# Two normalisation loops of a transformer layer, issued one and two tiles apart

## What is computed

```python
def _layernorm(x, axis=-1, eps=1e-5):
    m = jnp.mean(x, axis=axis, keepdims=True)
    v = jnp.var(x, axis=axis, keepdims=True)
    return (x - m) / jnp.sqrt(v + eps)
# attention: 16 heads of 64, causal, rope on q and k
qkv = einsum('bsd,ed->bse', x, W_qkv)
out = softmax(mask(rope(q) @ rope(k).T / 8)) @ v
return einsum('bsd,ed->bse', out, W_o)
# feed-forward: the input is normalised a second time inside
z = (x - mu) * rsqrt(var + EPS) * ln_g + ln_b
z_sent = mean(z, axis=1)
z_bn = (z_sent - bn_mean) * rsqrt(bn_var + EPS) * bn_g + bn_b
probs = softmax(z_bn @ Wr + br); idx = argmax(probs); gate = probs[idx]
h = relu(z @ W_down[idx] + b_down[idx])
y = (h @ W_up[idx] + b_up[idx]) * gate
# layer
x = x + attention(_layernorm(x))
x = x + ffn(_layernorm(x), ...)
```

## Time and profile before

| | us |
|---|---|
| median of 2 runs | 6524.79 |
| lowest, highest | 6509.48, 6540.09 |
| the profiled execution | 6517.81 |
| span of its slowest core (core 3) | 6516.3 |
| span of its fastest core (core 6) | 6481.7 |

### The profile page before, as it was taken

The page is one execution under the profiler, slowest core; times in us unless marked ns, Lnnn a source line. Parts: engine busy times, 40 slices in busy tenths (PEclk is TensorE's granted clock), DMA queues, the critical chain, the costliest instruction groups (busy, mean ns, idle before and its releaser), DMA issues. The chain is left out here.

```text
span 6516.3 us, 47310 instructions; the slowest of 8 cores (6481.7 to 6516.3 us)
## 1 busy us (share of the span) xinstructions
PE 4396.2 (67%) x11412; PEld 1075.9 (17%) x11412; DVE 2256.1 (35%) x2561; ACT 1701.7 (26%) x1983; POOL 1428.2 (22%) x1736
## 2 busy tenths in 40 slices
PE   0166888885346788888335688888634678888833
PEld 0022111111112111112002211111201221111200
DVE  1244323333434333333343433333334433332334
ACT  0000444430000244442000044444000014444300
POOL 0027000002225400000340810000123460000033
PEclk9989555556568755556557955555656985555655
DMA  5310000001021000002021100000202100000101
GB/s 140 113 36 17 1 0 1 1 30 39 16 100 28 9 1 1 1 0 68 0 87 42 23 1 1 1 1 1 68 2 105 34 12 1 0 1 1 62 7 62
DMA packets 151776, 180.51 MB, mean 28 GB/s; under 512 B 89951, under 2 KB 110559, under 8 KB 151015
## 3 DMA queue, kind: packets, MB, share of 16 engines
q1 hardware_dynamic: 151532, 177.48, 8.8%
HBM read 133.41 MB, written 44.04 MB: 27 GB/s over the span
## 5 line engine op out<-in xcount | busy, mean ns | idle before, releaser
L578 ACT ACTIVATE PT<-pss,ecol_s 128x1024 bf16<-128x1024 f32 x1280 | 1426.7, 1115 | 2451.2 <-PE pss L560 2447.2
L525 DVE RECIPROCAL rb<-po 64x512 f32<-64x512 f32 x256 | 859.9, 3359 | 2229.4 <-PE po L515 2229.4
L560 PE MATMUL pss<-qkT 64*128 64x512 bf16 x2560 | 1315.6, 616 | 0.0
L493 PE MATMUL po<-PT,v 128*65 128x512 bf16 (+3 forms) x2560 | 1225.0, 565 | 35.7 <-POOL PT L593 34.2
L593 POOL TENSOR_SCALAR_AFFINE_SELECT PT<-PT 128x128 bf16<-128x128 bf16 x1024 | 274.7, 292 | 2969.6 <-ACT PT L578 2969.0
L515 PE MATMUL po<-lr,ones_s 1*64 1x512 f32 x512 | 494.5, 1066 | 380.6 <-ACT lr L508 380.6
L427 PE MATMUL psq<-u1T,wqk 128*128 128x512 bf16 x2048 | 485.6, 381 | 219.0 <-DVE t1b L440 219.0
L787 PE MATMUL psz<-t,ones_s 128*1 128x512 f32 x256 | 228.2, 1045 | 482.8 <-DVE t L779 482.8
L369 PE MATMUL ptr<-ident_s,u1b 128*128 128x128 bf16 x512 | 64.1, 303 | 630.0 <-DVE u1b L357 630.0
L453 POOL TENSOR_TENSOR t2b<-qks,ropeB_s 128x512 f32<-128x512 f32 x256 | 324.5, 1268 | 716.7 <-DVE t1b L440 680.6
L493 PEld LDWEIGHTS po<-PT,v 128*65 128x65 bf16 x2560 | 274.5, 140 | 1190.2 <-issue 1166.8
(11 more groups left out here) (94 smaller groups left out, 2164.0 us busy)
## 6 DMA issues: line engine op xcount, KB each, us to landing
xb<-x SPq DMA_DIRECT2D x64, 512.0 KB, 3.9
xr<-x SPq DMA_DIRECT2D x64, 512.0 KB, 4.0
out<-x2o SPq DMA_DIRECT2D x64, 512.0 KB, 2.6
wqk<-wqk_b SPq DMA_DIRECT2D x64, 256.0 KB, 3.0
cbuf_f<-wqk SPq DMA_DIRECT2D x16, 512.0 KB, 4.7
wvb<-wv_b SPq DMA_DIRECT2D x32, 256.0 KB
wob<-wo_b SPq DMA_DIRECT2D x32, 256.0 KB
wqk_b<-cbuf_b SPq DMA_DIRECT2D x16, 256.0 KB, 2.8
```

The source lines that it names most:

```text
L493: e.matmul(pso[i_hqb % 2][0:65, sigma:512], vsb[:, j * NH * 66 + h * 66: j * NH * 66 + h * 66 + 65], PT[:, sl4 * 512 + sigma: sl4 * 512 + ...
L525: e.reciprocal(rb[sl][:, :], posb[sl][64:128, :])
L560: e.matmul(pss[sl2][:, (jj % 2) * 512: (jj % 2) * 512 + 512], qkT[hb:hb + 64, kcol + jj * 128: kcol + (jj + 1) * 128], qkT[hb:hb + 64, qco ...
L578: e.activation(PT[:, slot0 * 512: slot0 * 512 + 1024], pss[sl2][:, :], AF.Exp, bias=self.ecol[:, 1:2], scale=0.125) \
```

## The change

Both loops are cut into functions per step, and the steps of different tiles are interleaved. In p1 the loop issues load, statistics and Ln/Exp of tile t, then `u1b`, transposes and their copy of tile t-1, then V of tile t-2. In p3 it issues the first statistics and Ln/Exp of tile t, then `u2b`, second statistics and Ln/Exp of tile t-1, then `t3b`, column sums, `gz`/`zb`, transposes and copy of tile t-2. For this `stat6`, `mv`, `rstd`, `u2b` and `st6` get two buffers. Room comes from `gz` in bf16 and from `R_bup`, which now shares the place of `R_zs`. ScalarE and GpSimd get semaphores of their own (`s_cha`, `s_chg`) in place of `s_ch`, and the first statistics of p3 wait in addition for VectorE's own second statistics of tile t-2.

```diff
@@ p1
-                stat6 = self.sb(sca, f"st6_{s}", [128, 12], F32)
-                mv = self.sb(sca, f"mv_{s}", [128, 2], F32)
-                rstd = self.sb(sca, f"rs_{s}", [128, 1], F32)
+                stat6 = [self.sb(sca, f"st6_{s}_{i}", [128, 12], F32)
+                         for i in range(2)]
+                mv = [self.sb(sca, f"mv_{s}_{i}", [128, 2], F32) for i in range(2)]
+                rstd = [self.sb(sca, f"rs_{s}_{i}", [128, 1], F32)
+                        for i in range(2)]
...
                 for t in range(NT):
...
+                    st_load(t)
+                    st_stats(t)
+                    st_rstd(t)
                     if t >= 1:
-                        plan_v(t - 1)
+                        st_apply(t - 1)
+                        st_tr(t - 1)
+                        st_evac(t - 1)
+                    if t >= 2:
+                        plan_v(t - 2)
+                st_apply(NT - 1)
+                st_tr(NT - 1)
+                st_evac(NT - 1)
+                plan_v(NT - 2)
                 plan_v(NT - 1)
@@ p3
-            u2b = [self.sb(sc, f"u2{s}", [128, D], F32)] * 2
+            u2b = [self.sb(sc, f"u2{s}_{i}", [128, D], F32) for i in range(2)]
...
-            gz = self.sb(sc, f"gz{s}", [128, D], F32)
-            st6 = self.sb(sc, f"st6b{s}", [128, 12], F32)
+            gz = self.sb(sc, f"gz{s}", [128, D], BF16)
+            st6 = [self.sb(sc, f"st6b{s}_{i}", [128, 12], F32)
+                   for i in range(2)]
...
-            R_bup = rows[:, D:2 * D]
-            o3 = 2 * D
+            R_bup = R_zs
+            o3 = D
...
+                def q_s1(t):
+                    sl = t % 2
                     c0 = self.s_ch.inc()
-                    self.add("vector", lambda e, t=t, sl=sl, c0=c0: (
+                    wp = V2.get(t - 2, 0)
+                    V1[t] = self.s_stat.inc()
+                    self.add("vector", lambda e, t=t, sl=sl, c0=c0, wp=wp: (
+                        e.wait_ge(self.s_stat.h, wp) if wp else None,
...
+                for t in range(NT):
+                    q_s1(t)
+                    q_r1(t)
+                    if t >= 1:
+                        q_s2(t - 1)
+                        q_r2(t - 1)
+                    if t >= 2:
+                        q_t3(t - 2)
+                        q_zmm(t - 2)
+                        q_z(t - 2)
+                        q_ztr(t - 2)
+                q_s2(NT - 1)
+                q_r2(NT - 1)
+                for t in (NT - 2, NT - 1):
+                    q_t3(t)
+                    q_zmm(t)
+                    q_z(t)
+                    q_ztr(t)
```

More of the change, by code:

```diff
@@ L109, in build @@
                          "vmm vev smm exp msk pvmm lrow bc norm womm x1 st ch w0b st2 "
-                         "ldxb ldwb ldw3 ldw3b "
+                         "ldxb ldwb ldw3 ldw3b cha chg "
                          "t3 zmm z ztr zT gat sel hrelu ymm t2 x2 misc macc"
@@ new lines, in st_stats @@
+                def st_stats(t):
+                    sl = t % 2
+                    lsem = self.s_ldx if sl == 0 else self.s_ldxb
+                    w_ld = lsem.n
+                    c1 = self.s_ch.inc()
+                    self.s_stat.inc()
+                    self.add("vector", lambda e, sl=sl, ls=lsem, w=w_ld, c1=c1: (
+                        e.wait_ge(ls.h, w),
+                        e.bn_stats(stat6[sl][:, 0:6], xbuf[sl][:, 0:512]),
+                        e.bn_stats(stat6[sl][:, 6:12], xbuf[sl][:, 512:1024])
+                         .then_inc(self.s_ch.h, 1),
+                        e.wait_ge(self.s_ch.h, c1),
+                        e.bn_aggr(mv[sl][:, :], stat6[sl][:, :])
+                         .then_inc(self.s_stat.h, 1)))
@@ new lines, in st_apply @@
+                def st_apply(t):
+                    sl = t % 2
+                    w_tr = b_tr + t - 1 if t >= 2 else 0
+                    self.s_u1.inc()
+                    self.add("vector", lambda e, sl=sl, w=b_rstd + t + 1,
+                             w2=w_tr: (
+                        e.wait_ge(self.s_rstd.h, w),
+                        e.wait_ge(self.s_tr.h, w2) if w2 else None,
+                        e.tensor_scalar(u1buf[sl][:, :], xbuf[sl][:, :],
+                                        mv[sl][:, 0:1], rstd[sl][:, 0:1],
+                                        ALU.subtract, ALU.mult)
+                         .then_inc(self.s_u1.h, 1)))
@@ new lines, in st_tr, with _tr @@
+                def st_tr(t):
+                    sl = t % 2
+                    w_ev = b_ev + t if t >= 1 else 0
+                    self.s_tr.inc()
+                    def _tr(e, sl=sl, w=b_u1 + t + 1, w2=w_ev):
+                        e.wait_ge(self.s_u1.h, w)
+                        if w2:
+                            e.wait_ge(self.s_u1T.h, w2)
+                        for c in range(DC):
+                            ins = e.transpose(ptr[sl][:, c * 128:(c + 1) * 128],
+                                              u1buf[sl][:, c * 128:(c + 1) * 128],
+                                              self.ident[:, :])
+                        ins.then_inc(self.s_tr.h, 1)
+                    self.add("tensor", _tr)
@@ L361, in p1 @@
[L361 to L372, removed]
```

193 lines of the change are left out of this document (101 added, 92 removed).

## The result

| | before | after |
|---|---|---|
| median, us | 6511.4 (10 runs) | 6312.2 (11 runs, 6301.1 to 6339.1) |
| ratio, 95% interval | | 0.9696 [0.9676, 0.9717] |
| span of the profile's core, us | 6516.3 (core 3) | 6342.6 (core 4) |
| first stage, 4 sequences, us | 673.9 | 620.2 |
| p3, 4 sequences, us | 870.5 | 734.9 |

A forecast was written before the change was run, and what follows sets the result against it. The prediction took the first stage and p3 as chains handed from engine to engine, no engine full. From the profiled 6517.8 us it took 111 (p3's ACT waits) and 6 (first stage), the rest 0: 6401 us, range 6335 to 6440.

The forecast's parts named there:

- (a): p3: both DVE waits for ACT vanish, 1.73 us a tile, -111 us, at most -117; the wait for POOL stays.
- (b): p3: `gz` in bf16 leaves `zb` at 2.34 us, judged by L593; 0 us.
- The bounds of -75 and +15: p3, `gz` in bf16: -75 us if `zb` took half its time, +15 if conversion on reading cost a tenth.
- (c): First stage: 0.94 us ACT trip goes, but the clock's raster keeps tiles at 10.24; -6 us, bounds 0 and -60.
- rival 2: First stage gives its trip too: 9.3 us a tile, 6351 us, chance 0.22; clock never falling, 6270, chance 0.03.
- The ends of the loop: First stage: V of tile 0 some 1.5 us later per sequence, last interval 1.6 shorter; together 0.
- (d): Own semaphores for ACT and POOL, shared rows buffer, one more DVE wait in p3's first statistics: 0 us.

The follow-up runs named there:

- the fillers: Changed kernel plus unread VectorE statistics over 96, 256, 512 or 768 elements per first-stage tile: 6369.2, 6350.3, 6340.5, 6383.8 us.
- 512 more elements: Changed kernel plus one unread VectorE bn_stats over 512 elements per first-stage tile, ahead of its own statistics: 6340.5 us.
- the kernel with the doubled buffers: Changed kernel with two PSUM buffers for V, the V copy one tile later and a third x buffer: 6046.8 us, ratio 0.9299.
- the two kernels: Changed kernel with p3's transposes ahead of column sums, zT copy later: 6044.3 us; that p3, `u` moved, plus doubled first-stage buffers: 5739.6 us.

## Why the prediction was wrong, and where it was right

**(a) p3's ACT waits: right.** Forecast 111 us, at most 117. The trips start to start are 0.87 and 0.89 us shorter, 1.76 a tile, 113 us over 64 tiles. The stage as a whole gave 136, over that bound, by the two items that follow. DVE stops where the prediction said it would, at the `zT` copy of the same tile.

**(b) `zb` at 0: a term mis-sized.** It is 0.21 us a tile cheaper, 13 us; the kernel with `gz` in bf16 alone shows 12 in the stage. The row I went by, L593, reads one bf16 tensor and not two tensors, and said nothing of this. The bounds of -75 and +15 held.

What else p3 gave, some 11 us, goes with the clock: the transposes run at 2.4 GHz more often (0.61 us for the eight, and 1.01 at 1.2 GHz), in 102 of 176 tiles where it was 39, and a tile is 11.30 or 11.71 us long according to that, where it was 13.30 or 13.70. The prediction had no term for it. So tiles are 2.15 us shorter and not 1.73, and the copies came 11.5 apart where 12.0 was forecast.

**(c) The steady tile of the first stage unchanged at 10.24: the step that failed.** The prediction saw the period rightly, as the fillers show, down to bursts that lengthen as the gap shortens. But it extended it to a gap that no row covered. In the earlier trace rows the bursts shift against the rises of the clock by 3 us, and I read this as room for 0.94. In all these tiles the gap of PE had one length, 4.76 us. The rows varied the burst's position and never the gap's length, and the change varies the gap.

The sentence that broke is that the burst comes 0.94 sooner "after a clock that has fallen". The trace of before contradicts it in the very tile that I had read (core 3, columns as before):

```profile
5088.30:5092.50 4.20, 0.00 (x0) 0.00 (x0) 3.20 (x5) 0.50 (x2) 0.00 (x0) 1.00 0.00 0
5092.60:5093.00 0.40, 0.01 (x1) 0.04 (x2) 0.14 (x1) 0.00 (x0) 0.00 (x0) 0.50 0.00 0
```

The clock fell at about 5092.5 and the transposes began at 5092.99, so 0.94 us sooner is before the fall. Measured, the transposes of after take under 0.8 us in 118 of 176 tiles where 3 did before, and in 35 the clock does not fall at all. The early start alone does not end the period, since with 512 more elements 121 tiles have it too; the tiles without a fall come with its end. They account for about half of the loss: without them the mean of after is 9.96. PE's timeline on core 4, the tile of 8.00 us shown above and the next:

```profile
4873.71 0.61 PE L353 MATMUL ptr<-ident_s,u1b 128*128 128x128 bf16 x8 [3.87 <-DVE u1b L338]
4874.16 3.62 PE L384 MATMUL psv<-wvb,u1T 128*128 128x512 bf16 x16
4881.64 0.71 PE L353 MATMUL ptr<-ident_s,u1b 128*128 128x128 bf16 x8 [3.87 <-DVE u1b L338]
4882.14 5.24 PE L384 MATMUL psv<-wvb,u1T 128*128 128x512 bf16 x16
```

The period is still kept at 4.20 us of gap, and the change goes to 3.87. The 44 steady intervals on a core at 0.82 us each are 36 us. This is rival 2, to which I gave 0.25 in all; that its 9.3 us a tile lies near the 9.57 measured is chance. The 9.57 is a mixture: tiles of 7.93 in which the clock never fell, beside tiles of 9.6 to 10.8. The Trainium skill (TensorE: Matmul & The Clock Gate, Part 1) has it that activity is what releases the low clock; the tile at a clock of 1.00 agrees, and so does the kernel with the doubled buffers, whose gap is 1.0 us.

**The ends of the loop: mis-sized.** The prediction let the start cost 1.5 us and the last interval gain 1.6, together nothing. The load of tile 2 did stall DVE, by 2.3 us on average, and the first V copy came 1.25 us later in each sequence: 5 us lost. The interval that loses its statistics is the last but one and not the last, which is 5.1 us in most sequences before and after. It went from 10.47 on average to 6.89 (6.4 to 8.5 us), 14 us in all and over twice what its statistics take, as the gap in it is 2.31 us. The first two intervals, which are not counted as steady, gave another 9. Together that is the other 18 of the 54 us.

**(d) Semaphores and rows buffer: nothing, as forecast,** as far as a remainder of 8 us can say it.

**In sum**, of the 89 us missed, 48 lie in the first stage and 25 in p3. The remainder is 8 us in no stage followed, and 7 us because the sum was made from a profiled execution of 6518 us and the median then measured for before was 6511. The rule that the Trainium skill gives for POOL (GPSIMD Engine Reference, section 3.1), that the two inputs take turns at one read port, I had read as "the width does not matter"; 2132 ns for 2339 disagree with that reading.

## What to carry to other kernels

Issuing loops a tile apart removes the waits between short operations, but the long wait stays with, or moves to, the next list that still follows its newest tile: here in p3 first DVE's copy, then PE's column sums, and in the first stage the only PSUM tile. Go through the list of every engine, and every tile that has one buffer, before you price such a change. With all three opened the kernel is about 760 us faster than before, nearly four times the 198 of the change alone. And where a stage keeps a fixed period that its instructions do not explain, a trace in which the idle gap has one length cannot tell how far a shorter gap still keeps it: add a filler and measure. And where the clock falls inside that gap, read how near to its end: here it was about 0.5 us ahead of it, and 0.9 us less of gap began most bursts before the fall.

## What the hardware showed that I had not expected

- The loop of gap and V burst in this kernel has a mean period of 10.23 us at gaps of 4.20 and 4.46 us and 10.40 at 4.8, and 9.57 at 3.87. From 3.87 to 4.20, 0.33 us more work costs 0.66 us a tile, and from 4.20 to 4.46 nothing.
- VectorE's f32 `tensor_scalar` from SBUF to SBUF, 0.79 us alone, takes up to 2.75 us beside a tensor-tensor of GpSimd, and mostly ends 0.55 us after it. The statistics beside it keep their 0.68 us and the copies out of PSUM their 0.69. The Trainium skill (SBUF — State Buffer, section SBUF: two separate sides) says that the port pair which the two engines share is held for a whole instruction by whichever starts first, a GpSimd operation or a VectorE operation that needs both ports, and the other waits. The rows of the two kernels agree with the wait, at 0.55 and 0.56 us behind the other's end; on who is first the row at 5906.05 does not fit to the letter, as `u` is recorded 0.02 us ahead of the `zb` that it waits for. Moving `u` to where `zb` has ended was not tried.
- A GpSimd tensor-tensor of 128x1024 with one bf16 input takes 2132 ns for 2339.
- The output projection runs at a lower clock on some cores. After, on cores 4 and 0 (columns as before):

```profile
5997.00:6061.00 64.00, 60.84 (x249) 25.85 (x247) 21.26 (x20) 0.16 (x1) 0.00 (x0) 0.88 0.38 121
```

```profile
5952.00:6008.00 56.00, 53.44 (x241) 24.05 (x244) 20.49 (x18) 0.00 (x0) 0.00 (x0) 0.99 0.42 134
```

At 0.88 for 0.99, 64 us hold about the work of 56. This is the scatter that the section on the result names. What brings it on is not shown.
